# Weighted cross attention: the values' bias folded into the output bias once, the values copied by ACT in place of DVE

## The reference, cut to what matters

```python
q = (queries @ Wq.T + bq).reshape(B, Nq, h, d).transpose(0, 2, 1, 3)
k = (keys @ Wk.T + bk).reshape(B, -1, h, d).transpose(0, 2, 1, 3)
v = (values @ Wv.T + bv).reshape(B, -1, h, d).transpose(0, 2, 1, 3)
scores = jnp.einsum('bhqd,bhkd->bhqk', q, k) / jnp.sqrt(jnp.float32(d))
...
```

## Time and profile before

| | |
|---|---|
| median of 3 runs | 2589.75 us (2586.35 to 2591.84) |
| the profiled execution | 2593.18 us, span 2591.4 us |
| mean granted TensorE clock | 0.98 |
| phase A1 | about 552 to 1010 us of the span |

### The profile page before, as it was taken

How to read it: one execution, slowest core, us unless ns; L and a number is a source line. 1 busy time by engine, 2 the same in 40 slices (tenths; PEclk the granted TensorE clock), 3 DMA queues, 4 the chain that set the end, 5 groups by cost and what they waited for, 6 DMA issues and landing times. The chain is left out here.

```text
span 2591.4 us, 83416 instructions
## 1 busy us (share of the span) xinstructions
PE 2355.9 (91%) x26926; PEld 1806.6 (70%) x26926; DVE 1894.2 (73%) x4003; ACT 1498.3 (58%) x3407; POOL 1539.6 (59%) x2438
## 2 busy tenths in 40 slices
PE   6999998987777777999998988999999999999899
PEld 4666666975656565777776876777777777777587
DVE  4676764139999994677776667888888888888566
ACT  4777775558888884777776542444444444444333
POOL 2555555127888884455556776666666666666332
PEclk9999999989999997999999998999999999999999
DMA  4111111235555551222121223333333333333111
GB/s 121 38 38 39 36 40 44 71 109 153 148 155 148 154 153 39 51 46 46 47 47 41 65 63 83 92 94 97 97 95 95 94 94 96 94 94 93 50 58 54
DMA packets 443043, 211.78 MB, mean 82 GB/s; under 512 B 206400, under 2 KB 433856, under 8 KB 442816
## 3 DMA queue, kind: packets, MB, share of 16 engines
q1 hardware_dynamic: 442944, 210.51, 30.7%
HBM read 113.36 MB, written 29.88 MB: 55 GB/s over the span
## 5 line engine op out<-in xcount | busy, mean ns | idle before, releaser
L666 PE MATMUL bank<-sb_ident,sb_region 128*77 128x128 f32 x3072 | 413.8, 278 | 85.7 <-ACT sb_pT L754 84.8
L666 PEld LDWEIGHTS bank<-sb_ident,sb_region 128*77 128x77 f32 x3072 | 350.2, 151 | 139.9 <-issue 137.7
L754 ACT ACTIVATE sb_pT<-bank 77x1024 f32<-77x1024 f32 x384 | 391.6, 1020 | 67.1 <-PE bank L666 67.0
L858 DVE TENSOR_REDUCE sb_max<-bank 128x8 f32<-128x616 f32 x256 | 203.5, 795 | 205.8 <-PE bank L648 118.0
L1528 ACT ACTIVATE sb_l<-sb_l 128x640 f32<-128x640 f32 x128 | 94.5, 738 | 386.2 <-DVE sb_l L1576 386.2
L749 ACT ACTIVATE sb_region<-sb_region 128x616 f32<-128x616 f32 x384 | 276.8, 721 | 1.4 <-POOL sb_region L995 1.4
L1649 POOL TENSOR_TENSOR sb_pn<-sb_l,sb_r_all 128x512 f32<-128x512 f32 x128 | 134.7, 1052 | 233.4 <-DVE sb_r_all L1586 229.5
L1398 PE MATMUL bank<-sb_region,sb_wqkv 128*128 128x128 f32 x2048 | 255.2, 279 | 1.6 <-DVE sb_region L1564 0.8
L682 PE MATMUL bank<-sb_pT,sb_v 77*32 77x128 f32 x6144 | 248.2, 279 | 3.6 <-ACT sb_pT L754 3.2
L1438 PE MATMUL bank<-sb_wvo,sb_region 128*64 128x512 f32 x1024 | 248.0, 605 | 0.0
L1398 PEld LDWEIGHTS bank<-sb_region,sb_wqkv 128*128 128x128 f32 x2048 | 243.6, 195 | 4.1 <-DVE sb_region L1564 1.5
(11 more groups left out here) (183 smaller groups left out, 5645.4 us busy)
## 6 DMA issues: line engine op xcount, KB each, us to landing
sb_region<-in_side SPq DMA_DIRECT2D x64, 616.0 KB, 3.8
sb_pT<-sb_region SPq DMA_DIRECT2D x512, 64.0 KB, 2.1
sb_kF<-sb_region SPq DMA_DIRECT2D x512, 64.0 KB, 2.1
scratch_after_A<-sb_y SPq DMA_DIRECT2D x256, 64.0 KB, 1.8
sb_fx<-scratch_after_A SPq DMA_DIRECT2D x96, 128.0 KB, 2.1
sb_mask<-in_mask SPq DMA_DIRECT2D x64, 154.0 KB, 2.2
sb_x<-scratch_after_F SPq DMA_DIRECT2D x128, 64.0 KB, 1.9
sb_ctx<-in_ctxT SPq DMA_DIRECT2D x192, 38.5 KB, 1.9
```

Of the source, the lines that this page charges most:

```text
L666: mm = nc.tensor.transpose(two[0:C, h * T:(h + 1) * T], p_s[b.par][:, head * C:(head + 1) * C], ident[:])
L754: nc.scalar.activation(pT_s[k][:], two[0:C, :], ACT.Copy).then_inc(pT_kept.sem(b), 1)
L858: nc.vector.tensor_reduce(dst, by_bank_and_head(scores_half(k)), AX.X, ALU.max).then_inc(max_made.sem(b), 1)
```

## The change

`bv` of layer L1 is held as one column (128 partitions of one value). At the start of F0, DVE spreads it over 128 columns (`value_bias`, in a tile that is only used later). Between F0 and A1, PE multiplies it once with `wo`, and DVE adds the product to `bo`. In A1, `keep_v` is taken out of DVE's step and ACT's `keep_v`, a plain copy, is called in its step, behind `block_keys(b + 2)` and ahead of `centre(b - 3)`.

```diff
@@ the weights
             if ph != "A2":
                 w |= {k: column(p + k) for k in ("bq", "bk")}
+            if ph == "A0":
                 w["bv"] = row_everywhere(p + "bv")
-            if ph == "A0":
                 w["bo"] = w["bv"]
             else:
                 w["wo"] = weight(p + "wo", [D, D], a[p + "wo"])
                 w["bo"] = row_everywhere(p + "bo")
+            if ph == "A1":
+                w["bv"] = column(p + "bv")
@@ cross_scalar, step
                     block_keys(b + 2) if weighted else keep_k(b + 2)
                 if weighted:
+                    if has(1):
+                        keep_v(b + 1)
                     if has(-3):
                         centre(b + -3)
@@ cross_vector
-            def keep_v(b):
-                dve.wait_ge(v_made.sem(b), v_made.count(ph, b))
-                wait_earlier(dve, att_made, ph, b, 2, 1)
-                dst = v_s[b.par][:].rearrange("p (h v) -> p h v", v=VPAIR // 2)[:, :, 0:DH]
-                src = v_bank[0:C, V_COL:V_COL + D].rearrange("p (h v) -> p h v", v=DH)
-                nc.vector.tensor_tensor(dst, src, w["bv"][0:C, :].rearrange("p (h v) -> p h v", v=DH), ALU.add).then_inc(v_kept.sem(b), 1)
-
@@ cross_vector, step_weighted
                 if has(-1):
                     normalise(b + -1)
-                if has(1):
-                    keep_v(b + 1)
                 if has(-2):
                     sums(b + -2)
@@ between F0 and A1
+        value_bias = l_s[0][:, 0:T]
         def turn_sums(pe):
             pe.wait_ge(ctx_summed.sems[0], NB)
+            pe.wait_ge(masks_made, 6)
+            nc.tensor.matmul(bank[2][:, 0:D], value_bias, cross["A1"]["wo"][:], start=True, stop=True)
             nc.tensor.transpose(turn_bank[0:NB, 0:D], sumT[:], ident[:]).then_inc(sums_turned, 1)
         def pool_vector(dve):
             dve.wait_ge(sums_turned, 1)
+            bias = cross["A1"]["bo"]
+            nc.vector.tensor_tensor(bias[:], bank[2][:, 0:D], bias[:], ALU.add)
@@ before_ff, at the start of F0
+                nc.vector.tensor_copy(value_bias, cross["A1"]["bv"][:, 0:1].to_broadcast([D, T])).then_inc(masks_made, 1)
```

## The result

The changed kernel takes 2599.95 us as the median of 7 runs (2595.76 to 2604.33), against 2591.34 us for the kernel before (7 runs, 2586.35 to 2595.20). The ratio is 1.0036, with a 95% interval of 1.0023 to 1.0049: slower, by 8.6 us. The forecast was 2599.2 us and +0.36%, worked out as 9.4 us on top of the 2589.75 us of the first three runs of the kernel before; over its seven runs that kernel's median is 2591.34 us. The profiled execution has a span of 2602.5 us, 11.1 us more than before.

A forecast was written before the change was run, and what follows sets the result against it. The prediction took ACT's unbroken work plus PE from scores to transpose_o to bound A1. 59 x 0.16 = 9.4 us for the copy, all else 0, on the 2589.75 us median gave 2599.2 us (+0.36%), range 2591 to 2607.

The forecast's parts named there:

- What bounds A1: A1's steady steps: ACT and PE waiting for each other set the 6.77 us mean period; DVE does not.
- The ring: One A1 step: 4.44 us of ACT, 0.58 us to the scores, 1.67 us of PE, 6.69 us in all.
- ACT's unbroken stretch: ACT in A1 from keep_att to keep_q without idle time: 4.44 us, to become 4.60 us.
- The price of the copy: ACT's added copy of the values in A1: 0.16 us in each of 59 steps, 9.4 us.
- the row of A2: Same copy instruction on ACT in A2: lasts 0.27 us, next instruction starts 0.16 us after it; taken as the price.
- No gap for it: ACT ahead of keep_pT(b, 1) in A1: centre already used up the wait for PE's transposes, so no gap hides the copy.
- The one-off work and the placement: Product and addition between F0 and A1, spread copy in F0, tiles' new places in SBUF: each taken as 0.
- DVE's idle time after: DVE ahead of the weighting in A1: idle time grows from 29.3 us by 59 x (0.16 + 0.20), to about 50 us.
- DVE reaches the wait for the scores that much sooner and waits longer: DVE in A1 without its addition: 0.20 us sooner at the wait each step, taken as 0 for the time.
- DVE was the bound: Rival: DVE's chain sets A1's period, so losing 0.20 us a step saves 11.8 us, giving 2578 us; chance 0.05.

The follow-up runs named there:

- early q: keep_pT(b, 1) moved behind keep_q and keep_xT in A1: from the kernel before 2565.89 us (ratio 0.9896), from the changed kernel 2558.32 us (0.9868).

## Why the prediction was right

*What bounds A1.* Right. The ring of ACT's unbroken stretch, the scores and `transpose_o` set the period. The stretch went from 4.44 to 4.60 us with one copy and 4.76 with two, and to 4.23 us with `centre` out of it, and the period went along each time. DVE's addition, taken away without ACT's copy or put back beside it, moved nothing: 399.7 against 399.6 us, and 408.8 against the 410.1 us of the changed kernel less its fall of 0.9 us.

*The price of the copy.* Right in size: 0.16 us a step from the row of A2. The Trainium skill's figures (page "ScalarE: Activation LUTs", section "What ACT_TABLE_LOAD costs") gave an estimate of 0.20 us; the step in this trace is 0.15 to 0.16 us, so the measurement decides. The copy itself lasts 0.27 to 0.29 us here. That the forecast time came within 0.8 us is in part luck: 9.4 us stand against a measured 8.6 us, on a base that lay 1.6 us lower than the later median.

*No gap for it.* Right, and the experiment with `centre` late shows the point from which it would have been otherwise: with 0.16 us of wait ahead of `keep_pT(b, 1)` the change costs 1.2 us.

*The one-off work and the placement.* Taken as 0, and 0.9997 (0.9988 to 1.0006) bears it out for both together.

*DVE's idle time after.* Wrong. The step that failed is "DVE reaches the wait for the scores that much sooner and waits longer". It reaches the mask sooner and is held there until POOL's subtraction is over. That did not touch the forecast time, since DVE hangs beside the ring, but the rival "DVE was the bound" was priced too high by it: at this place in the order, 0.20 us taken from DVE brings its weighting no nearer. In the order with early q the relief of DVE was worth 6.2 us after all, by way of POOL, which no rival of the prediction had.

*What the forecast left out.* The fall of the granted clock, 0.9 us in the profiled execution. With one copy more the falls were some 5.4 of the 25.6 us by which the 59 periods exceed those of before.

## What to carry to other kernels

Busy shares say which engine is loaded, not which one is paid for: look for the stretch that runs without idle time from one releaser to the next, and price a moved instruction at its start-to-start step, full if it enters such a stretch and nothing if a wait stands behind it there. The same move that cost 9 us in one order gained 6 to 8 us in another, so after a reordering it is worth trying again what was a loss. And a little more idle time on PE can cost more than the wait itself, when its granted clock falls.

## What the runs showed of the hardware

- DVE's masking (two SBUF inputs, 128 x 616) takes 0.79 us early in the step. Where its record starts 0.19 us or more behind the start of a POOL subtraction of 1.22 us (also 128 x 616), it is drawn out and ends 0.65 us behind POOL's end: 1.45 us when it starts 0.42 us behind, 1.64 us when it starts 0.23 us behind. Where DVE's record starts first, by 0.06 to 0.14 us, it is POOL that takes 1.76 to 1.81 us and ends about 1.07 us behind the end of the mask. Where DVE's starts up to 0.15 us behind POOL's, it goes one way or the other: POOL then takes 1.86 to 2.02 us, or DVE 1.77 to 1.87 us. In each such pair one engine seems to stand still while the other works.
- With two copies on ACT, a period of 7.1 us in place of 6.8 and the same work on PE, the granted clock fell from 2.4 to 1.2 GHz for 3 us six times in 59 steps. With PE busy for 333 of 392 us in place of 298 it did not fall. The two needless products, 0.71 us of PE in each step, made the kernel 10 us faster, some 5 to 6 us of it by the clock.
